# The router of a mixture of experts: moments in three groups, normalising and affine on ScalarE, choices and destinations for two batches at once

## What is computed

```python
hn2 = _layernorm(x, ln2_g, ln2_b).reshape(-1, h)       # 4096 tokens x 128
logits = hn2 @ gate_w + gate_b                         # 8 experts
idx = jnp.argmax(logits, axis=-1)
mid = jax.nn.relu(jnp.einsum('th,ehf->etf', hn2, w1) + b1[:, None, :])
y = jnp.einsum('etf,efh->eth', mid, w2) + b2[:, None, :]
moe = y[idx, jnp.arange(hn2.shape[0])]
return x + moe.reshape(b, s, h)
```

## Time and profile before

| what | us |
|---|---|
| three runs | 2310.29, 2315.4, 2316.72 |
| their median | 2315.4 |
| the profiled execution, its own time | 2313.86 |
| its span in the profile | 2312.2 |
| `moe` in the span: first instruction to the last load issued | 853.2 to 1037.2 |
| of it the router, to the first load of a sorted tile | 853.2 to 922.4 |

### The profile page before, as it was taken

How to read it: one execution, slowest core, us unless ns; L and a number is a source line. 1 busy time by engine, 2 the same in 40 slices (tenths; PEclk the granted TensorE clock), 3 DMA queues, 4 the chain that set the end, 5 groups by cost and what they waited for, 6 DMA issues and landing times. The chain is left out here.

```text
span 2312.2 us, 54874 instructions
## 1 busy us (share of the span) xinstructions
PE 1908.8 (83%) x18758; PEld 832.9 (36%) x18758; DVE 1678.7 (73%) x3088; ACT 1202.4 (52%) x2297; POOL 1159.2 (50%) x712
## 2 busy tenths in 40 slices
PE   6367544699999964986995999999999999999985
PEld 3267422122222224662442233333333333333333
DVE  7922486777878737434563889888888898888856
ACT  5321111377777740213663466666666666666655
POOL 8533542000000007330002588888888888888877
PEclk9688666689999985997997899999999999999995
DMA  1310035111111113116886222222222222222201
GB/s 44 48 25 1 8 103 157 49 34 42 33 41 33 34 61 116 48 52 209 286 285 193 68 75 75 75 74 68 67 70 75 75 75 74 74 68 68 74 4 44
DMA packets 243077, 179.60 MB, mean 78 GB/s; under 512 B 59764, under 2 KB 230900, under 8 KB 242692
## 3 DMA queue, kind: packets, MB, share of 16 engines
q1 hardware_dynamic: 235140, 172.38, 26.5%
q0 software_dynamic: 2304, 4.74, 0.6%
q10 hardware_dynamic: 5504, 0.73, 0.2%
HBM read 101.16 MB, written 75.26 MB: 76 GB/s over the span
## 5 line engine op out<-in xcount | busy, mean ns | idle before, releaser
L919 DVE TENSOR_REDUCE maxima_l<-max_l 128x1 f32<-128x512 f32 x1024 | 673.7, 685 | 119.4 <-PE max_l L995 108.8
L959 ACT ACTIVATE probs_l<-exp_l 128x512 f32<-128x512 f32 x1024 | 580.4, 600 | 320.8 <-PE exp_l L1008 308.8
L892 POOL TENSOR_TENSOR part_sums_l<-probs_l 128x1024 f32<-128x1024 f32 x256 | 623.6, 2436 | 163.5 <-ACT probs_l L959 153.2
L995 PE MATMUL max_l<-k_stack_l,q_stack_l 96*128 96x512 f16 x1024 | 401.3, 392 | 42.9 <-DMA k_stack_l<-scratch_qk_l 25.6
L1008 PE MATMUL exp_l<-q_stack_l,k_stack_l 100*128 100x512 f16 x1024 | 388.4, 381 | 0.0
L1203 DVE TENSOR_REDUCE maxima_l<-max_l 128x2 f32<-128x1024 f32 x256 | 305.5, 1222 | 88.6 <-PE max_l L1287 87.4
L1239 ACT ACTIVATE probs_l<-exp_l 128x512 f32<-128x512 f32 x512 | 282.8, 598 | 120.3 <-PE exp_l L1301 119.5
L1043 PE MATMUL pv_bank_l<-probs_l,v_ring_l 128*32 128x512 f32 x2048 | 273.4, 606 | 0.3 <-issue 0.3
L995 PEld LDWEIGHTS max_l<-k_stack_l,q_stack_l 96*128 96x128 f16 x1024 | 98.9, 97 | 429.4 <-DVE maxima_l L919 383.6
L1641 POOL IOTA rows_e<- 128x32 int32 x1 | 0.2, 188 | 446.4 <-POOLq L26 446.4
L898 POOL TENSOR_TENSOR part_sums_l<-part_sums_l 128x512 f32<-128x512 f32 x128 | 183.3, 1432 | 10.0
(11 more groups left out here) (271 smaller groups left out, 2608.1 us busy)
## 6 DMA issues: line engine op xcount, KB each, us to landing
scratch_qk_l<-parts_g SPq DMA_DIRECT2D x128, 256.0 KB, 2.2
q_stack_l<-scratch_qk_l SPq DMA_DIRECT2D x192, 128.0 KB, 2.7
k_stack_l<-scratch_qk_l SPq DMA_DIRECT2D x192, 128.0 KB, 2.7
scratch_v_l<-v_g SPq DMA_DIRECT2D x32, 512.0 KB, 3.5
v_ring_l<-scratch_v_l SPq DMA_DIRECT2D x64, 256.0 KB, 2.9
scratch_stack_l<-parts_c SPq DMA_DIRECT2D x96, 128.0 KB, 2.3
q_stack_l<-scratch_stack_l SPq DMA_DIRECT2D x64, 96.0 KB, 2.1
k_stack_l<-scratch_stack_l SPq DMA_DIRECT2D x64, 96.0 KB, 2.1
```

The costliest lines, as they stand in the source:

```text
L892: pool.tensor_tensor(part_sums[:, i, h, :, :], probs[:, i, h, 0:2, :], probs[:, i, h, 2:4, :], ALU.add).then_inc(pair_sum.sem, 1)
L919: dve.reduce_max(maxima[:, s % 2, at % NT, at // NT:at // NT + 1], max_ps[at % 2][:, :], AX).then_inc(max_taken.sem, 1)
L959: act.activation(probs[:, i, at // NT, at % NT, :], exp_ps[exp_bank(s, at)][:, :], ACT.Exp, scale=a.scale).then_inc(prob_tile.sem, 1)
L995: pe.matmul(max_ps[at % 2][:, :], qs[0:SHIFT_ROW, s % RING, h, k * P:(k + 1) * P], ks[0:SHIFT_ROW, s % RING, h, :], start=True, stop=True) ...
```

## The change

- The moments are taken in the three groups of `NORM_GROUPS`, ahead of the rest of DVE's program, and no longer behind the wait for the weights. Each buffer of theirs holds all 32 tiles. POOL computes three powers (4, 12 and 16 columns) ahead of all scatters.
- `centre` on DVE computes `shift`; `normalise` and `affine` are ACT's now, as `activation(Identity)` with a scale and a bias per partition.
- The logits of two batches stand side by side in one bank, and each of the four pairs has a bank of its own (`mid_bank`, `midT_bank`, idle in the router). `score` no longer waits for `choose`. `rank` takes a pair, in two banks in turn, and the counts go to `zT_bank[0]`.
- `choose`, `destine` and `scatter` work on a pair: operations on 64 columns in place of 32, eight dependent additions in place of four twice, eight scatters in a row.
- `tabulate`, `fill_tails`, the experts and SP's program are as they were.

```diff
-        logits_bank, rank_bank = y_bank
-        stats, mv = sb("stats", [P, 2, NT, 6]), sb("mv", [P, 2, NT, 2])
+        stats, mv = sb("stats", [P, T, 6]), sb("mv", [P, T, 2])
+        var_eps, rstd, shift = sb("var_eps", [P, T]), sb("rstd", [P, T]), sb("shift", [P, T])
...
+        PAIRS = B // 2
+        of_pair = lambda p: slice(p * 2 * NT, (p + 1) * 2 * NT)
+        logits_bank, rank_bank, count_bank = [*mid_bank, *midT_bank], y_bank, zT_bank[0]
...
-            for i in range(B + 2):
-                if i < B:
-                    reciprocal_std(i)
-                if i >= 2:
-                    scatter(i - 2)
+            for n in range(len(NORM_GROUPS)):
+                pool.wait_ge(moments.sem, moments.made(n, 0))
+                size = tiles_of(n).stop - tiles_of(n).start
+                pool.tensor_tensor(rstd[:, tiles_of(n)], var_eps[:, tiles_of(n)], g.minus_half[:, 0:size], ALU.pow).then_inc(rstd_ready.sem, 1)
+            for p in range(PAIRS):
+                scatter(p)
...
+            def centre(n):
+                tiles = tiles_of(n)
+                dve.wait_ge(rstd_ready.sem, rstd_ready.made(n, 0))
+                dve.scalar_tensor_tensor(out=shift[:, tiles], in0=mv[:, tiles, 0], scalar=-1.0, in1=rstd[:, tiles],
+                                         op0=ALU.mult, op1=ALU.mult).then_inc(shift_ready.sem, 1)
...
+            take_moments(0)
+            take_moments(1)
+            centre(0)
+            take_moments(2)
+            centre(1)
+            centre(2)
             dve.wait_ge(w_loaded, 16 * 4)
             dve.wait_ge(built, 8)
...
+            for p in range(PAIRS):
+                choose(p)
+                destine(p)
             tabulate()
...
+            def normalise(b):
+                act.wait_ge(shift_ready.sem, shift_ready.made(group_of(b), 0))
+                for k in range(b * NT, (b + 1) * NT):
+                    act.activation(rows[:, k, 0:D], g.z[:, k, :], ACT.Identity, bias=shift[:, k:k + 1],
+                                   scale=rstd[:, k:k + 1]).then_inc(zn_ready.sem, 1)
+
+            def affine(b):
+                act.wait_ge(zT_ps.sem, zT_ps.made(b, 0))
+                if b >= 2:
+                    act.wait_ge(logits_ps.sem, logits_ps.made(b - 2, 0))
+                act.activation(hT[:, b % 2, :], zT_bank[b % 2][:, :], ACT.Identity, bias=col[:, 1:2], scale=col[:, 0:1]).then_inc(hT_ready.sem, 1)
+
+            act.wait_ge(ids_ready, 1)
+            act.wait_ge(w_loaded, 16 * 4)
+            normalise(0)
+            for b in range(B):
+                if b + 1 < B:
+                    normalise(b + 1)
+                affine(b)
             act.wait_ge(zeros_ready, 2)
             fill_tails(act, range(E_ // 2, E_))
...
-                if b:
-                    pe.wait_ge(chosen.sem, chosen.made(b - 1, 0))
...
+            transposes(0)
+            for b in range(B):
+                if b + 1 < B:
+                    transposes(b + 1)
+                score(b)
+                if b >= 2 and b % 2 == 0:
+                    rank(b // 2 - 1)
+            rank(PAIRS - 1)
+            pe.matmul(count_bank[:, 0:E_], ones[:, :], before[:, T, :], start=True, stop=True).then_inc(counted, 1)
```

More of the change, by code:

```diff
@@ L1599, in fill_tails @@
                 eng.dma_start(scratch.sorted[bass.ds(at, P), :], zeros[:, e, :]).then_inc(zeroed, 16)
+        group_of = lambda b: [n for n, (first, end) in enumerate(NORM_GROUPS) if first <= b < end][0]
+        tiles_of = lambda n: slice(NORM_GROUPS[n][0] * NT, NORM_GROUPS[n][1] * NT)
+        PAIRS = B // 2
+        of_pair = lambda p: slice(p * 2 * NT, (p + 1) * 2 * NT)
+        logits_bank, rank_bank, count_bank = [*mid_bank, *midT_bank], y_bank, zT_bank[0]
+        by_tile = lambda bank: bank[:, 0:2 * NT * E_].rearrange("p (k e) -> p k e", e=E_)
         block = ctx.enter_context(nc.Block())
@@ L1695, in settle, with take_moments @@
                 dve.wait_ge(own, mine[0])
-            z = lambda b, k: g.z[:, b * NT + k, :]
-            def take_moments(b):
-                if b >= 2:
-                    dve.wait_ge(rstd_ready.sem, rstd_ready.made(b - 2, 0))
-                for k in range(NT):
-                    did(dve.bn_stats(stats[:, b % 2, k, :], z(b, k)))
+            def take_moments(n):
+                tiles = tiles_of(n)
+                for k in range(tiles.start, tiles.stop):
+                    did(dve.bn_stats(stats[:, k, :], g.z[:, k, :]))
@@ L1705, in take_moments @@
                 settle()
-                for k in range(NT):
-                    did(dve.bn_aggr(mv[:, b % 2, k, :], stats[:, b % 2, k, :]))
+                for k in range(tiles.start, tiles.stop):
+                    did(dve.bn_aggr(mv[:, k, :], stats[:, k, :]))
                 settle()
-                dve.tensor_scalar(var_eps[:, b % 2, :], mv[:, b % 2, :, 1], LN_EPS, None, ALU.add).then_inc(moments.sem, 1)
-            def normalise(b):
-                dve.wait_ge(rstd_ready.sem, rstd_ready.made(b, 0))
-                for k in range(NT):
-                    dve.tensor_scalar(rows[:, b * NT + k, 0:D], z(b, k), mv[:, b % 2, k, 0:1], rstd[:, b % 2, k:k + 1],
-                                      ALU.subtract, ALU.mult).then_inc(zn_ready.sem, 1)
@@ L1717, in affine @@
-            def affine(b):
-                dve.wait_ge(zT_ps.sem, zT_ps.made(b, 0))
-                dve.tensor_scalar(hT[:, b % 2, :], zT_bank[b % 2][:, :], col[:, 0:1], col[:, 1:2], ALU.mult, ALU.add).then_inc(hT_ready.sem, 1)
-            def choose(b):
-                at = slice(b * NT, (b + 1) * NT)
-                dve.wait_ge(logits_ps.sem, logits_ps.made(b, 0))
-                did(dve.tensor_tensor(logits[:, :, :], logits_bank[:, 0:NT * E_].rearrange("p (k e) -> p k e", k=NT),
-                                      gate_b[:, :].unsqueeze(1).broadcast_to([P, NT, E_]), ALU.add))
+                dve.tensor_scalar(var_eps[:, tiles], mv[:, tiles, 1], LN_EPS, None, ALU.add).then_inc(moments.sem, 1)
@@ new lines, in centre, with choose @@
+            def centre(n):
+                tiles = tiles_of(n)
+                dve.wait_ge(rstd_ready.sem, rstd_ready.made(n, 0))
+                dve.scalar_tensor_tensor(out=shift[:, tiles], in0=mv[:, tiles, 0], scalar=-1.0, in1=rstd[:, tiles],
+                                         op0=ALU.mult, op1=ALU.mult).then_inc(shift_ready.sem, 1)
+            def choose(p):
+                dve.wait_ge(logits_ps.sem, logits_ps.made(2 * p + 1, 0))
+                did(dve.tensor_tensor(logits[:, :, :], by_tile(logits_bank[p]),
+                                      gate_b[:, :].unsqueeze(1).broadcast_to([P, 2 * NT, E_]), ALU.add))
@@ L1734, in choose @@
                 settle()
-                did(dve.tensor_tensor(choice[:, at, :], logits[:, :, :], bc(best[:, :], E_), ALU.is_equal))
+                did(dve.tensor_tensor(choice[:, of_pair(p), :], logits[:, :, :], bc(best[:, :], E_), ALU.is_equal))
                 settle()
-                for k in range(b * NT, (b + 1) * NT):
+                for k in range(of_pair(p).start, of_pair(p).stop):
                     last = dve.tensor_tensor(before[:, k + 1, :], before[:, k, :], choice[:, k, :], ALU.add)
-                    if k + 1 < (b + 1) * NT:
+                    if k + 1 < of_pair(p).stop:
                         did(last)
@@ L1753, in destine @@
                 settle()
-                dve.tensor_copy(dest[:, at], placed[:, :]).then_inc(dest_ready.sem, 1)
+                dve.tensor_copy(dest[:, of_pair(p)], placed[:, :]).then_inc(dest_ready.sem, 1)
             def tabulate():
                 dve.wait_ge(counted, 1)
-                did(dve.tensor_copy(count[:, :], logits_bank[:, 0:E_]))
+                did(dve.tensor_copy(count[:, :], count_bank[:, 0:E_]))
                 settle()
```

68 lines of the change are left out of this document (21 added, 47 removed).

## The result

| | median us | runs | ratio to before, 95% |
|---|---|---|---|
| before | 2313.95 (2310.29 to 2316.72) | 4 | |
| changed | 2335.17 (2332.29 to 2338.54) | 4 | 1.0089 [1.0071, 1.0107] |

The change makes the kernel 0.9% slower, some 20 us. The forecast was 2312.2 with a range of 2307 to 2318: wrong, and on the wrong side.

A forecast was written before the change was run, and what follows sets the result against it. The zeros, late behind DVE's chain, ended SP's wait; afterwards POOL's scatters would. First scatter 876.1, last ending 917.0, plus 1.35 and 0.8 gives first load 919.2 instead of 922.41: 3.2 us earlier, median 2315.4 to 2312.2, range 2307 to 2318.

The forecast's parts named there:

- Bound of the stage: End of the router: the zeros' stores end SP's wait before the change, POOL's last scatter after it.
- First scatter: Router, POOL: the first scatter starts at 876.1, where it started at 870.38 before.
- the second score: Router, PE: the scores of the first pair's second batch are done at 870.5.
- the terms given for the moments: Router, DVE: groups of 4, 12 and 16 tiles cost 1.4, 3.7 and 4.6 us, together given as 9.7.
- Scatters: Router, POOL: 31 steps of 1.26 us, 39.1 us, with 0.46 added for slow ones; the last ends at 917.0.
- rival 2: Router: DVE's work beside 20 scatters slows POOL, chain 6.6 us longer, kernel 3.4 us slower, 2318.8; chance 0.08.
- The powers that no longer stand between scatters: Router, POOL: seven of eight powers leave the scatter chain, offset by a start 5.7 us later.
- Release of SP: Router's end: SP is let go 1.35 us after the last scatter and loads 0.8 us later, at 919.2, 3.2 us earlier.
- Behind that nothing changes: After the first sorted tile's load: experts and later stages keep their times, so the 3.2 us reach the end.
- slower: Whole kernel: measurably slower, by DVE hindering POOL's scatters with an unlucky median; chance 0.04.
- the stage's own rivals: Router: DVE's time is the gain, 2301 (0.05); DVE hinders POOL, 2318.8 (0.08); first pair late, 2315.4 at 879.3 (0.09).

The follow-up runs named there:

- e15: Changed kernel with the announced branch and the first pair of batches made ready earlier (moments in groups of 8, 8, 16 tiles); 2314.2 us, ratio 0.9995 to the kernel before.
- e17: e15's kernel with 11 idle products on PE while it waits for the first sorted tile; 2311.8 us, ratio 0.9978 to the kernel before.
- e1: Changed kernel with DVE's loop head in the second layer's attention at slot 0 of a fetch block; 2319.8 us in one execution.
- e9: Changed kernel with 83 one-column memsets on DVE behind the table, moving its later loop; 2321.6 us, ratio 1.0036 to the kernel before.
- e10: Kernel before, router untouched, with DVE's attention loop at slot 200 of a block of 256; 2332.7 us, ratio 1.0082.
- e11: Kernel before, router untouched, with DVE's attention loop at slot 176 of a block of 256; 2322.8 us in one execution.
- e2: Changed kernel with ACT's loop head in the second layer's attention at slot 0, DVE's loop as it lies; 2327.0 us.
- e3: Changed kernel with both DVE's and ACT's attention loop heads at slot 0; 2313.8 us, ratio 0.9998 to the kernel before.
- e5: Changed kernel with empty instructions (83 DVE, 28 PE) that the build dropped, so the changed kernel again; 2332.0 us, ratio 1.0079 to the kernel before.
- e6: Changed kernel with 28 empty instructions on PE that the build dropped, so the changed kernel again; 2323.7 us in one execution.
- e8: Changed kernel with the next turn's branch announced at the top of each attention loop turn on DVE and ACT; 2308.8 us in one execution.
- e13: Changed kernel with the announced branch in the attention loop on DVE and ACT, timed; 2316.9 us, ratio 1.0005 to the kernel before.
- e14: Kernel before with the same announced branch in the attention loop; 2317.7 us, ratio 1.0008 to the kernel before without it.
- e12: Changed kernel with the announced branch on DVE and ACT and DVE's attention loop at slot 200; 2320.6 us in one execution.
- e16: e13's kernel with 11 idle products on PE while it waits for the first sorted tile; 2313.5 us, ratio 0.9993 to the kernel before.
- e18: e13's kernel with 22 idle products on PE while it waits for the first sorted tile; 2313.2 us, ratio 0.9983 to the kernel before.

## Why the prediction was wrong, point by point

**Bound of the stage: right.** SP's wait was ended by the zeros before, and is by the last scatter after. The stores of the zeros are issued from 897.4 to 901.3 in the trace, 895.7 to 899.6 with the 1.7 us off (898 to 906 forecast), SP's wait for them ends at 905.3, and the table is ready at 898.9 with the shift off (902).

**First scatter: right.** 875.4 with the shift taken off, against 876.1. The terms behind it: `affine` on ACT measured 0.76 to 0.78 us, I took 0.7; the second score started at 867.9 so counted and ran 1.71, so it ended at 869.6 against 870.5. A slip in the sum is part of it: the terms given for the moments make 9.5 us and not 9.7, and 9.5 is what they took (855.02 to 864.54).

**Scatters: right, and rival 2 did not come.** 32 at 1.26 with no wait between pairs. The first took 1.23, all others 0.95 to 0.96, beside DVE's `choose` too: DVE did not hinder them. I had taken the rule of the Trainium skill's page "SBUF — State Buffer", section "Who interferes with whom", too far: it also says that `tensor_tensor` and `tensor_reduce` on DVE did not stall DMAs made by GpSimd. This chain agrees: behind the first, no scatter is longer. The last ended at 915.7, against 917.0: I had added 0.46 us for slow scatters that were not there, and my start was 0.7 late. The powers that no longer stand between scatters are five, by the order shown, and not seven; the sum has no term for them.

**Release of SP: right.** 2.1 us from the last scatter's end (917.44) to the first load (919.53), against 1.35 + 0.8. So the router gained 4.6 us against the profile shown of before, where I said 3.2; over all profiles without a stop it is 64.6 against 68.7 on average (six of the old router, 67.85 to 69.22; e15 and e17 left out), 4.1 us.

**"Behind that nothing changes": this step failed**, twice.

- In the second attention. The prediction took the change to end where its last instruction ends. It also changes how many instructions DVE and ACT have ahead of everything that follows, and with them the place of a loop of 327 instructions on DVE. DVE waits 2.5 us at six turns, 15.3 us in all; the waits go when only the loop's place is changed (e1, e9), and appear in the kernel before in the same way (e10, not e11). I had counted instructions by what they cost where they run, never by where they put the code behind them, and no rival was a later stage.
- In the experts. The stage's length is no constant to which a gain can be added. One program gave 119.2, 118.8 and 111.4 us. All six profiles of the old router lie from 111.0 to 117.1 (mean 114.2), the eight of the changed one without a stop (changed kernel, e1, e2, e3, e5, e6, e8, e13) from 111.4 to 120.6 (mean 116.5). Router and experts together are 182.9 and 181.1: of 4.1 us, 1.8 are left on average, less than the spread. Timing says the same: e13 and e14 differ by 0.0003. How much of the difference in the experts is systematic stays open. The meeting of packet and scatter is systematic where it falls, but late loads are as many before as after, two per profile, so it isn't shown to be what takes the router's gain away.

The gain of the router lay within its bounds (4.1 to 4.6 us, against 3.2 with 0.3 to 5.3), the sign of the whole was wrong, and the certainty was the worst part: I gave 0.04 to "slower" because the stage's own rivals were weak, though nothing in my views reached behind 1037 us.

## What to carry to other kernels

A change to straight-line code moves all loops behind it. Before giving a later stage nothing, count each engine's instructions ahead of its large loops before and after; where a body is larger than one block, pin its place or announce its branch, and do it in both kernels before comparing them, or the comparison times the code's place. And look for waits for "issue" that recur at the turns of a loop, with the instruction packets of the page: two lines that told it here at once.

A gain ahead of a stage that runs in a closed ring of buffers and DMAs is first of all an earlier start; here 1.8 of 4.1 us reached the end on average, within the spread. Take the spread of the stage from repeated profiles before adding such a gain.

## What was not expected of the hardware

- A loop that reaches into a third block costs DVE 2.5 us at each turn, with five more packets of 8 KB in each, and nothing when it ends 24 places earlier (e10, e11).
- An announced branch takes the wait away and, which I can't explain, the repeated packets too: 44 to 47 in place of 75 to 104 (e8, e12, e13). In e12 one wait of 2.7 us is left.
- A single instruction packet of 16 KB that starts 1.0 to 1.75 us after an indirect store is issued makes the next step hear of the store late in 36 of 40 cases, by some 1.4 us at the ninth load (3.34 against 4.7 to 5.3 us).
- In two of fourteen profiles of the changed router with its variants (e9 and e12, on the same chip, where e16 to e18 later had none) DVE stood still twice in the router, at the same two instructions, with POOL scattering on meanwhile until it ran out of destinations. In e9:

```profile
888.37 0.23 DVE L1739 TENSOR_TENSOR place_e<-y_ps_e,region_e 128x64 f32<-128x64 f32 x1 [6.82 <-issue]
...
900.30 0.23 DVE L1717 TENSOR_TENSOR logits_e<-midT_ps_e,gate_b_e 128x64 f32<-128x64 f32 x1 [10.82 <-DMA q_stack_l<-shift_l]
```
```profile
905.84 1.17 POOL L1669 DMA_INDIRECT scratch_sorted<-rows_e,dest_e  x1 [4.94 <-DVE dest_e L1746]
```

  The router then takes 69.8 us (69.6 in e12), the 5 us of POOL's wait more. It would fit e9's ratio of 1.0036, if most of its executions had it, which wasn't measured. The score that the second of DVE's rows reads had left PE at 884.3. The cause is open; no packet of instructions is recorded for that time.
